# Two-layer sequence model on one core: the last batch's end in halves of two tiles, and a quarter of the low one-hots made by GpSimd and gathered last

## The chip, the cores and the metric

The kernel runs as one program on one core of one Trainium2 chip. The metric is the device time of one execution in microseconds (us). Engines are named as in the profile: PE (TensorE, matmul), PEld (its weight loads), DVE (VectorE), ACT (ScalarE), POOL (GpSimd), SP (SyncE, which only issues DMAs here). There is one core, so every semaphore wait below is between engines of the same core.

## What is computed

Input x is 4 batches of 512 tokens by 128 features. Four sublayers follow one another, each with a residual and a LayerNorm without weights. The last two matter here.

```python
# third sublayer: causal linear attention, 16 heads of 8
numer = einsum(q, cumsum(k v)); denom = max(einsum(q, cumsum(k)), 1e-6)
y = numer / denom;  x3 = layernorm(x2 + y @ w_out.T)
# fourth: product-key expert layer, 8192 rows of down and up, 8 heads, top 8
mean, var = x3 over all 2048 tokens, per feature           # batch norm
xn = (x3 - mean) * rsqrt(var + eps) * bn_gamma + bn_beta
sim = (xn @ w_q.T) . keys                                  # 2 sides x 8 heads x 32 keys
scores, idx = top_k(sim, 8)                                # first choice, per side
all_scores = scores[0][:, None] + scores[1][None, :]
sc, pk = top_k(all_scores, 8)                              # second choice, 64 rows a token
indices = 32 * idx[0] + idx[1] at pk                       # numbers below 8192
h = gelu(x3 . down[indices]) * sigmoid(sc)
out = layernorm(x3 + sum(h * up[indices]))
```

The batch norm needs the moments of all four batches, so the fourth sublayer cannot start before x3 of the last batch is done.

## The kernel before, in words

The program is two blocks, one after the other: `layers` (the first three sublayers, about 290 us of the span) and `peer` (the fourth). Within a block each engine has its own instruction list, written out by hand in a fixed order; engines meet only in semaphore waits (`wait(engine, semaphore, b, k)`). There is no planner. At the end of a block all engines wait for one another.

**End of `layers`.** A batch has T = 4 tiles of 128 tokens. The last batch (B - 1 = 3) ends with a serial chain over all four tiles: VectorE reduces the numerators (`b_summed`, line 984) and makes y (`b_y`, 988 to 993); TensorE transposes y (`b_yt`, 1428); ScalarE copies it out (502); TensorE multiplies with w_out (`b_z3`, 1435); VectorE adds x2 (`b_z3`, 1000) and takes the moments of each row (`b_z3_spread`, 791 to 796); GpSimd raises to the power -1/2 (`root`, 625); VectorE normalises to x3 (`b_x3`, 801); TensorE transposes x3 (`b_x3t`, 1443); ScalarE copies (507); VectorE takes the batch norm's moments of the copy (`b_moments`, 1016). Then `peer` begins with `bn_aggr` (2028), a root on GpSimd and, on ScalarE, `xn` (`normed`, 1770).

**`peer`.** A pair is two tiles (256 tokens); there are PAIRS = 8 pairs p, with tiles u = 2p and 2p + 1. Looking up rows of down and up is done with one-hot matmuls and no gather: a number below 8192 is split into a low part (0 to 127) and a high part (below 64). For each of the 128 chosen slots of a token ("lanes" in the code) there is a low one-hot of 128 columns and a high one-hot weighted with the sigmoid; their product over tokens' lanes, taken on TensorE, has 128 by 8 entries per token. The low one-hots of a pair are made in QB = 4 quarters of LB = 32 lanes. VectorE makes quarters 0 to 2 in one instruction each (`hot_lo`, 1970). ScalarE makes quarter 3 (`last_one_hots`, 1814 to 1827): 32 Abs activations, one per lane, then one Relu over all of them, with the Gelus of `hidden` put in between the lanes ("meanwhile") in pairs 2 to 5. In pair 7 ScalarE makes 16 of those lanes and VectorE the other 16 (`last_lanes`).

The order of one pair on each engine:

- VectorE: `one_hots(p)` (lo_last 1946, w_lo 1948, lo_t, hot_hi, hot_w, then hot_lo three times), `residual(p-1)` (moments of the output, 2019 to 2025), `second_choice` of both tiles of pair p+1 (1900, 1903), `rows_columns` (1911 to 1918), `which_side` (1924), `weigh(p)` (mix, 2007; first half after two gathered quarters, second half after four), `first_choice` of both tiles of pair p+2 (1889, 1893).
- TensorE: quarters 0, 1, 2 gathered (`gathered`, 2137) with one product of `hidden` (2084) ahead of each in pairs 2 to 5; `key_scores(2p+4)` (2073); quarter 3; `key_scores(2p+5)`; one more hidden product in pairs 2 to 5; `decoded(p+1)` (2100); `outputs(p)` (2148, 2150), which waits for o of the pair before.
- ScalarE: `decoded(p)` (1809 to 1812), `side_numbers` (1793), `last_one_hots(p)`, `normal(p-1)` (o, 1835), the copies of the two key scores (`keysims`, 1778), `sigmoids` (1801), the fourth Gelu.
- GpSimd: `root(p-1)` (1738, 1741), `numbers` (eq, 1730), `candidates` (1716, 1720). It waits for the most part.
- SP: one store of a pair's output after o.

`first_choice(u)` cannot start before the copy of `key_scores(u)`; `decoded(p+1)` waits for `numbers` and `sigmoids`; the outputs of pair 7 wait for o of pair 6.

## Time and profile before

| | |
|---|---|
| three runs | 540.2, 542.76, 550.87 us, median 542.76 |
| profiled execution | 542.56 us, span 540.8 us |
| mean granted TensorE clock | 0.766 of full speed |
| busy: PE, PEld | 390.4 us (72%), 271.0 us (50%) |
| busy: DVE, ACT, POOL | 467.1 us (86%), 300.4 us (56%), 184.5 us (34%) |
| chain that ended last | DVE 25%, PE 16%, ACT 2% of the span are named in it |

Times in a row are from the start of the span. A busy share is an average over both blocks; what bounds a pair is read from the timelines of one pair. In a timeline row the first number is the start, the second the length of the merged piece, and a bracket at its end gives the idle time of that engine ahead of it and what ended it.

### The profile page before, as it was taken

What the parts mean: (1) busy time and instruction counts of PE and PEld (TensorE: products, weight loads), DVE (VectorE), ACT (ScalarE), POOL (GpSimd) and SP (SyncE); (2) the same over time, 40 slices, a digit from 0 to 9 for tenths busy, and PEclk for the clock granted to TensorE, in tenths of its full rate; (3) what the DMA queues carried; (4) which work ended last, traced back from release to release, by engine and by line L of the source; (5) the groups of instructions that cost most, each with busy time, mean ns of one, the idle gap of its engine ahead of it and who ended that gap; (6) DMA issues with size and microseconds to landing.
All of it is one profiled execution on the core that took longest, in us unless ns stands there. A gap on an engine that the chain in (4) does not pass through costs nothing. (4 is left out here: it accounts for less than half of the span.)

```text
span 540.8 us, 16061 instructions
## 1 busy us (share of the span) xinstructions
PE 390.4 (72%) x6356; PEld 271.0 (50%) x6356; DVE 467.1 (86%) x2059; ACT 300.4 (56%) x625; POOL 184.5 (34%) x209
## 2 busy tenths in 40 slices
PE   2997579877798769776345846767887878785575
PEld 1662466555555555456342325555564545545575
DVE  5387998899978998997954999999999999999992
ACT  1433455186434754238421678483968787778551
POOL 3454229632683129423511540304040403040001
PEclk9999895999688996977555885757576765858577
DMA  4800000000000000000000000000000000000000
GB/s 93 235 34 0 1 1 2 2 1 1 1 2 1 1 1 2 1 1 1 2 1 0 1 1 4 4 14 2 4 13 2 13 3 14 2 13 2 13 3 21
DMA packets 12473, 6.95 MB, mean 13 GB/s; under 512 B 3182, under 2 KB 11758, under 8 KB 12398
## 3 DMA queue, kind: packets, MB, share of 16 engines
q1 hardware_dynamic: 11366, 5.65, 3.8%
q8 instruction: 50, 0.82, 0.6%
q10 hardware_dynamic: 1032, 0.27, 0.2%
q14 instruction: 25, 0.20, 0.1%
HBM read 4.87 MB, written 1.05 MB: 11 GB/s over the span
## 5 line engine op out<-in xcount | busy, mean ns | idle before, releaser
L1820 ACT ACTIVATE hot_last<-iota_f,lo_last 128x128 f16<-128x128 f32 x240 | 72.8, 393 | 0.3 <-DVE lo_last L1946 0.3
L2137 PE MATMUL psum<-hot_w,hot_lo 64*128 64x8 f16 x2688 | 39.7, 164 | 39.8 <-DVE hot_lo L1970 26.0
L2137 PEld LDWEIGHTS psum<-hot_w,hot_lo 64*128 64x128 f16 x2688 | 37.8, 101 | 56.4 <-DVE hot_lo L1970 29.9
L1970 DVE TENSOR_TENSOR hot_lo<-lo_t,iota_lo 128x4096 f16<-128x4096 f16 x24 | 53.5, 2285 | 0.0
L2084 PE MATMUL psum<-x3t,down_t 128*128 128x512 f32 x64 | 45.9, 842 | 1.7 <-PEq L319 1.7
L1730 POOL TENSOR_TENSOR eq<-eq,side_f 128x1024 f16<-128x1024 f16 x14 | 29.0, 2088 | 48.9 <-DVE eq L1924 48.9
L1893 DVE FIND_INDEX8 side_i<-side,keysims 128x8 uint32<-128x32 f32 x256 | 41.6, 192 | 0.0
L1300 PE MATMUL psum<-we,x1t 128*128 128x512 f32 x64 | 39.6, 731 | 2.3 <-DVE wexp L875 1.1
L1738 POOL TENSOR_TENSOR rstd<-rstd,minus_half 128x2 f32<-128x2 f32 x8 | 5.7, 707 | 104.3 <-DVE rstd L2025 104.3
L1386 PE MATMUL psum<-q_hi,k_t 32*128 32x128 f16 x256 | 21.2, 264 | 19.1 <-DVE masked L952 13.1
L679 POOL TENSOR_TENSOR s_lo<-feat,s_hi 128x512 f16<-128x512 f32 x28 | 31.7, 1159 | 8.6 <-ACT s_hi L487 8.6
L2150 PE MATMUL psum<-upw,mix 128*128 128x128 f32 x256 | 34.3, 292 | 0.0
L679 POOL TENSOR_TENSOR s_lo<-masked,s_hi 128x512 f16<-128x512 f32 x28 | 31.6, 1158 | 7.0 <-DVE x L801 3.7
L2150 PEld LDWEIGHTS psum<-upw,mix 128*128 128x128 f32 x256 | 33.3, 210 | 0.0
L2073 PE MATMUL psum<-keysim,xn 128*128 128x512 f32 x32 | 30.1, 1040 | 3.2 <-ACT keysims L1778 2.6
L889 DVE SCALAR_TENSOR_TENSOR z<-psum,wexp,z 128x128 f32<-128x128 f32 x112 | 29.6, 342 | 0.0
L1386 PEld LDWEIGHTS psum<-q_hi,k_t 32*128 32x128 f16 x256 | 12.8, 115 | 33.2 <-DVE masked L952 22.4
L487 ACT CAST s_hi<-feat 128x512 f16<-128x512 f32 x32 | 18.4, 618 | 19.5 <-PE psum L1419 14.3
L1889 DVE MAX8 side<-keysims 128x8 f32<-128x32 f32 x256 | 25.3, 187 | 3.7 <-ACT keysims L1778 3.7
L1827 ACT ACTIVATE hot_last<-hot_last 128x4096 f16<-128x4096 f16 (+1 forms) x8 | 27.2, 3404 | 0.3
L487 ACT CAST s_hi<-masked 128x512 f16<-128x512 f32 x32 | 19.2, 618 | 13.8 <-DVE masked L952 13.8
L625 POOL TENSOR_TENSOR a_rstd<-a_rstd,minus_half 128x2 f32<-128x2 f32 (+1 forms) x12 | 9.7, 805 | 49.7 <-DVE a_rstd L796 49.3
(281 smaller groups left out, 1113.2 us busy)
## 6 DMA issues: line engine op xcount, KB each, us to landing
xall<-in_L_attn_x SPq DMA_DIRECT2D x4, 256.0 KB, 4.6
out<-o SPq DMA_DIRECT2D x8, 128.0 KB, 1.8
we<-in_L_ffn_We SPq DMA_DIRECT2D x1, 512.0 KB, 4.3
downn<-in_L_ffn_down SPq DMA_DIRECT2D x1, 512.0 KB, 5.3
upw<-in_L_ffn_up SPq DMA_DIRECT2D x1, 512.0 KB, 6.3
wh<-in_L_attn_W_h SPq DMA_DIRECT2D x1, 256.0 KB, 3.2
keysn<-in_L_ffn_keys_p SPq DMA_DIRECT2D x1, 256.0 KB, 5.5
wqkv<-in_L_attn_w_qkv ACTq DMA_DIRECT2D x1, 192.0 KB
```

Source lines behind the costliest of these rows:

```text
L487: nc.scalar.copy(s_hi[:, u % 2, g, :], masked[u % 2][:, g, :]).then_inc(shi_ok.h, 1)
L679: nc.gpsimd.tensor_tensor(s_lo[:, u % 2, g, :], masked[u % 2][:, g, :], s_hi[:, u % 2, g, :], ALU.subtract).then_inc(slo_ok.h, 1)
L889: ins = nc.vector.scalar_tensor_tensor(z2[:, u, :], src, wexp[:, u, e:e + 1], (z2 if e else x1)[:, u, :], ALU.mult, ALU.add)
L1300: ins = nc.tensor.matmul(bank[Y_BANK[u] + k][:], x1t[:, P * u:P * u + P], v.we[:, 4 * k:4 * k + 4, :].rearrange("p e m -> p (e m)"), start ...
L1386: ins = nc.tensor.matmul(bank[S_BANK[b][g]][:, P * c:P * c + P], k_t[r, u, c, :], q[r, u, c, :], start=(q is q_hi), stop=(q is q_lo))
L1820: ins = nc.scalar.activation(hot_last[:, lane], iota_f[:], ACT.Abs, bias=lo_last[:, lane:lane + 1], scale=-1.0)
L1893: ins = nc.vector.max_index(side_i[:, u % 4, s, :], side[:, u % 4, s, :], keysims[:, u % 4, s, :])
L1970: nc.vector.tensor_tensor(hot_lo[:, pairs], bc(lo_t[:, lanes].rearrange("p (j s) -> p j s", s=2).unsqueeze(2), [P, LB // 2, P, 2]), bc(v.i ...
L2073: nc.tensor.matmul(bank[6][:], xn[:, P * (u % T):P * (u % T) + P], v.keysim[:].rearrange("p s k -> p (s k)"), start=True, stop=True)\
L2084: nc.tensor.matmul(bank[H_BANK(b, c)][:], v.down_t[:, c, :], v.x3t[:, N * b:N * b + N], start=True, stop=True).then_inc(h_mm.h, 1)
L2137: ins = nc.tensor.matmul(bank[2 + q // 2 * 2 + t][:, c:c + EH], low, hot_w[half, i, lane // 2, :, lane % 2], start=(lane % (2 * LB) == 0 a ...
L2150: ins = nc.tensor.matmul(outputs_of(p, t), mix[:, EH * t + e, :], v.upw[:, e, :], start=False, stop=(e == EH - 1))
```

## The change

In `layers`, the last batch is taken in halves of two tiles from y on. `b_y` takes a range of tiles; in the last batch it is called for tiles 0 and 1 right after `b_summed(1)` and for tiles 2 and 3 at the end. Transposes, copy, product, residual, moments, root, x3 and its transposes then run as two sets of half-size steps (`last_z3`, `last_yt`, `last_x3`, `last_x3t`), with banks of their own in PSUM. The moments of the batch norm are taken per half in all batches (`bn_raw` has two sets per batch), in the last one straight from PSUM, and the copy to x3t on ScalarE follows them.

In `peer`, quarter 2 of the low one-hots moves from VectorE to GpSimd: 32 `tensor_scalar` instructions a pair (`mid_one_hots`), one per lane, each comparing the row of 128 column numbers with a number per partition. GpSimd starts them when VectorE has made both of its quarters of the pair, and they come ahead of `root(p-1)`, `numbers` and `candidates` in its list. The order of the gathers on TensorE becomes 0, 1, 3, 2, for all pairs; `key_scores(2p+4)` stays ahead of the fourth gather, `key_scores(2p+5)` behind it. VectorE takes `first_choice(2p+4)` between the halves of mix. In pair 7 the products with x3 go ahead of the wait for the last mix. xn of the first batch is made in two parts, so that the first key scores need only the first. One semaphore (upw_ok) is folded into another (zeroed).

```diff
-                def b_y(b):
+                def b_y(b, tiles=slice(0, T)):
...
+                        b_summed(b, 1)
+                        b_y(b, slice(0, 2))
+                        b_summed(b, 2)
+                        b_summed(b, 3)
+                        b_y(b, slice(2, T))
+                for i in range(2):
+                    last_z3(i)
+                for i in range(2):
+                    last_x3(i)
+                for i in range(2):
+                    last_moments(i)
...
+                def last_yt(i):
+                    act.wait_ge(yt_mm.h, B + i)
+                    nc.scalar.copy(yt[:, 2 * P * i:2 * P * i + 2 * P], bank[2 + i][:, 0:2 * P]).then_inc(yt_ok.h, 1)
+                def last_x3t(i):
+                    act.wait_ge(x3t_mm.h, B + i)
+                    act.wait_ge(bn_ok.h, B + i)
+                    at = N * (B - 1) + 2 * P * i
+                    nc.scalar.copy(v.x3t[:, at:at + 2 * P], bank[i][:, 0:2 * P]).then_inc(x3t_ok.h, 1)
...
+    GATHER_ORDER = (0, 1, 3, 2)
...
+                def mid_one_hots(p):
+                    pool.wait_ge(lo_last_ok.h, p + 1)
+                    wait(pool, hot_ok, p)
+                    for lane in range(LB):
+                        ins = nc.gpsimd.tensor_scalar(hot_mid[:, lane], iota_f[:], lo_last[:, lane:lane + 1], None,
+                                                      ALU.is_equal)
+                    ins.then_inc(hot_mid_ok.h, 1)
...
                 for p in range(-1, PAIRS):
+                    if p >= 0:
+                        mid_one_hots(p)
                     if p >= 1:
                         root(p - 1)
...
-                    for q in range(QB - 1):
+                    for q in range(QB - 2):
...
                     if p >= 0:
-                        weigh(p)
+                        weigh(p, (0,))
                     if p + 2 < PAIRS:
-                        for u in (2 * p + 4, 2 * p + 5):
-                            first_choice(u)
+                        first_choice(2 * p + 4)
+                    if 0 <= p < PAIRS - 1:
+                        weigh(p, (1,))
+                    if p + 2 < PAIRS:
+                        first_choice(2 * p + 5)
...
+                    if p == PAIRS - 1:
+                        for t in range(2):
+                            nc.tensor.matmul(outputs_of(p, t), ident[:], v.x3[:, 2 * p + t, :], start=True, stop=False)
...
-                    for q in range(QB - 1):
-                        for c in early[q:q + 1]:
+                    for i, q in enumerate(GATHER_ORDER[0:QB - 1]):
+                        for c in early[i:i + 1]:
                             hidden(p // PB + 1, c)
                         gathered(p, q)
                     if p + 2 < PAIRS:
                         key_scores(2 * p + 4)
-                    gathered(p, QB - 1)
+                    gathered(p, GATHER_ORDER[QB - 1])
                     if p + 2 < PAIRS:
                         key_scores(2 * p + 5)
```

## Rows read from the trace of the kernel before

**Rows 1.** Chain of waits: starts of w_lo, pairs 0, 1, 2, 6 (start, length, what)

```profile
321.27 0.20 DVE w_lo L1948
...
348.54 0.20 DVE w_lo L1948
...
376.39 0.20 DVE w_lo L1948
...
492.14 0.20 DVE w_lo L1948
```

**Rows 2.** Timeline of VectorE, pair 3 (start, length, line, operation, count, idle before)

```profile
407.56 6.69 DVE L1970 TENSOR_TENSOR hot_lo<-lo_t,iota_lo 128x4096 f16<-128x4096 f16 x3
...
421.03 1.29 DVE L1924 TENSOR_TENSOR eq<-rc,iota_r 128x1024 f16<-128x1024 f16 x2
...
424.50 1.29 DVE L2007 TENSOR_TENSOR mix<-psum,hid 128x512 f32<-128x512 f32 x2 [0.98 <-PE psum L2137]
...
434.08 0.19 DVE L1946 SCALAR_TENSOR_TENSOR lo_last<-hi_t,number 128x32 f32<-128x32 f16 x1
```

**Rows 3.** Timeline of TensorE, pair 3: third gather, key scores, fourth gather

```profile
417.50 1.87 PE L2137 MATMUL psum<-hot_w,hot_lo 64*128 64x8 f16 x128
419.30 2.07 PE L2073 MATMUL psum<-keysim,xn 128*128 128x512 f32 x2
422.59 1.87 PE L2137 MATMUL psum<-hot_w,hot_last 64*128 64x8 f16 x128 [1.22 <-issue]
```

**Rows 4.** Timeline of ScalarE, pair 3: Relu, o, copy of the key scores

```profile
418.87 3.62 ACT L1827 ACTIVATE hot_last<-hot_last 128x4096 f16<-128x4096 f16 x1
422.39 0.79 ACT L1835 ACTIVATE o<-psum,shift,rstd 128x128 f32<-128x128 f32 x2
423.08 0.58 ACT L1778 COPY keysims<-psum 128x512 f32<-128x512 f32 x1
```

**Rows 5.** Timeline of ScalarE: the Relu of pairs 0 and 1

```profile
332.05 3.62 ACT L1827 ACTIVATE hot_last<-hot_last 128x4096 f16<-128x4096 f16 x1
...
358.40 3.62 ACT L1827 ACTIVATE hot_last<-hot_last 128x4096 f16<-128x4096 f16 x1
```

**Rows 6.** Groups of GpSimd by line and form (count, busy us, mean ns, idle before)

```profile
L1716 POOL TENSOR_TENSOR cand<-side 128x128 f32<-128x128 f32 x16 | 6.6, 413 | 37.9 <-DVE side L1889 37.9
...
L1738 POOL TENSOR_TENSOR rstd<-rstd,minus_half 128x2 f32<-128x2 f32 x8 | 5.7, 707 | 104.3 <-DVE rstd L2025 104.3
...
L1752 POOL TENSOR_SCALAR upw<-upw 128x1024 f32<-128x1024 f32 x1 | 2.8, 2787 | 0.1
L1741 POOL TENSOR_TENSOR shift<-shift,rstd 128x2 f32<-128x2 f32 x8 | 1.6, 197 | 0.6
```

**Rows 7.** One line's instructions on GpSimd: ns min/median/max, 128x512

```profile
L646 POOL TENSOR_SCALAR heads_t<-qk_t,gam,bet x8: 763/796/1302, 15.0 to 174.8; 128x512 f32<-128x512 f32 x8
```

**Rows 8.** Timeline of ScalarE, pair 6: table load and sigmoids

```profile
506.34 1.28 ACT L1801 ACT_TABLE_LOAD   x1
507.63 0.40 ACT L1801 ACTIVATE weight<-best 128x64 f32<-128x64 f32 x2
```

**Rows 9.** Timeline of TensorE: decoding of pair 7, first x3 products of its outputs

```profile
511.44 1.03 PE L2100 MATMUL psum<-ident_row,eq 128*128 128x128 f16 x8 [2.91 <-DVE eq L1935]
...
530.11 0.76 PE L2148 MATMUL psum<-x,ident 128*128 128x128 f32 x2 [1.20 <-DVE mix L1998]
```

**Rows 10.** Timeline of VectorE, pair 7: its three quarters

```profile
518.58 6.70 DVE L1970 TENSOR_TENSOR hot_lo<-lo_t,iota_lo 128x4096 f16<-128x4096 f16 x3
```

**Rows 11.** Timeline of VectorE: end of the last batch, the three waits

```profile
283.70 0.69 DVE L1000 TENSOR_TENSOR z<-x,psum 128x512 f32<-128x512 f32 x1 [3.96 <-PE psum L1435]
...
287.03 1.11 DVE L801 TENSOR_SCALAR x<-z,b_mv,b_rstd 128x128 f32<-128x128 f32 x4 [1.12 <-POOL b_rstd L625]
...
289.33 0.69 DVE L1016 BATCH_NORM_STATS2 bn_raw<-x3t 128x6 f32<-128x512 f32 x1 [1.19 <-ACT x3t L507]
```

**Rows 12.** Timeline of ScalarE: xn of the first batch

```profile
292.16 0.81 ACT L1770 ACTIVATE xn<-x3t,bn_shift,bn_scale 128x512 f32<-128x512 f32 x1 [1.13 <-DVE bn_shift L2038]
```

More of the change, by code:

```diff
@@ L613, in _ @@
                         b_values(a, 0)
-                    b_yt(b)
+                    if b < B - 1:
+                        b_yt(b)
                     if a + 1 < B:
@@ L1599, in _ @@
                             b_numerators(b, u)
-                    b_yt(b)
-                    if a + 1 < B:
-                        a_qk(a + 1)
-                        a_rest(a + 1)
-                    b_z3(b)
-                b_x3t(B - 1)
+                    if b < B - 1:
+                        b_yt(b)
+                        if a + 1 < B:
+                            a_qk(a + 1)
+                            a_rest(a + 1)
+                        b_z3(b)
+                for i in range(2):
+                    last_z3(i)
+                for i in range(2):
+                    last_x3t(i)
 def peer(nc, v):
@@ L1769, in normed @@
                         wait(act, ksim_mm, T * b - 1)
-                    nc.scalar.activation(xn[:], v.x3t[:, N * b:N * b + N], ACT.Identity, bias=bn_shift[:],
-                                         scale=v.bn_scale[:]).then_inc(xn_ok.h, 1)
+                    for part in (slice(0, N),) if b else (slice(0, P), slice(P, N)):
+                        nc.scalar.activation(xn[:, part], v.x3t[:, N * b:N * b + N][:, part], ACT.Identity,
+                                             bias=bn_shift[:], scale=v.bn_scale[:]).then_inc(xn_ok.h, 1)
                 def key_scores(u):
@@ L1819, in last_one_hots @@
                     for lane in range(ACT_LANES(p)):
-                        ins = nc.scalar.activation(hot_last[:, lane], iota_f[:], ACT.Abs, bias=lo_last[:, lane:lane + 1],
+                        ins = nc.scalar.activation(hot_last[:, lane], iota_f[:], ACT.Abs, bias=lo_last[:, LB + lane:LB + lane + 1],
                                                    scale=-1.0)
@@ L1994, in weigh @@
                     if p == PAIRS - 1:
-                        for q in range(QB):
-                            wait(dve, g_mm, p, q + 1)
+                        for i, q in enumerate(GATHER_ORDER):
+                            wait(dve, g_mm, p, i + 1)
                             lanes = slice(LB * q, LB * q + LB)
@@ L2002, in weigh @@
                         return
-                    for half in range(2):
+                    for half in halves:
                         wait(dve, g_mm, p, 2 * half + 2)
@@ L2068, in key_scores @@
                 def key_scores(u):
-                    wait(pe, xn_ok, u // T)
+                    pe.wait_ge(xn_ok.h, u // T + 2 if u else 1)
                     if u:
@@ L2135, in gathered @@
                                 half, c = slice(HK * t, HK * t + HK), EH * (lane % (2 * LB))
-                                low = hot_lo[half, lane // 2, :, lane % 2] if q < QB - 1 else hot_last[half, lane - LB * q, :]
+                                if q < QB - 2:
+                                    low = hot_lo[half, lane // 2, :, lane % 2]
+                                else:
+                                    low = (hot_mid, hot_last)[q - (QB - 2)][half, lane - LB * q, :]
                                 ins = nc.tensor.matmul(
                                     bank[2 + q // 2 * 2 + t][:, c:c + EH], low, hot_w[half, i, lane // 2, :, lane % 2],
-                                    start=(lane % (2 * LB) == 0 and i == 0), stop=(i == 1), skip_group_check=True)
+                                    start=(lane == LB * q and q in (0, 3) and i == 0), stop=(i == 1), skip_group_check=True)
                     ins.then_inc(g_mm.h, 1)
```

109 lines of the change are left out of this document (75 added, 34 removed).

## The prediction

> **What bounds the kernel now.** The profiled execution took 542.56 us (span 540.8), within 0.2 us of the median of the three runs, 542.76; the sum below is made against 542.56. I read the chain of waits first. In the expert layer it repeats once per pair of tiles, and the starts of w_lo mark the pairs [rows 1]: pair 0 takes 27.27 us, pair 1 27.85, pairs 2 to 5 take 115.75 together, 28.94 each, and pair 6 begins at 492.14. I write T for such a start.
>
> Then the timelines of one middle pair (T = 405.34), one engine at a time. VectorE makes three low one-hot quarters, works on, and has one visible wait, 0.98 us, before the second half of mix at 424.50; from there to the next pair's first operation at 434.08 it is busy, 9.58 us of mix and two first choices [rows 2]. That wait ends with the last quarter of gathers on TensorE, 422.59 to 424.5 [rows 3]. Those gathers could have begun at 421.37, when the key scores started at 419.30 were through; they waited for ScalarE, whose Relu over its own quarter ends at 418.87 + 3.62 = 422.49 [rows 3, 4]. So VectorE and the ScalarE-to-TensorE chain are nearly tied, and the ScalarE quarter is today hidden behind one key-score product and the third gather.
>
> **The change, part by part.** *VectorE* loses one of three hot_lo operations, 6.69 / 3 = 2.2 us a pair [rows 2], 17.7 us over eight pairs. That counts only where nothing else ends later.
>
> *Gather order 0, 1, 3, 2.* TensorE reaches its third gather at 417.50 in the middle pair [rows 3], but this is now ScalarE's quarter, not ready before 422.49. Nothing moves ScalarE earlier: its start (lo_last) and the Gelus between its lanes are as before. TensorE idles five us, gathers until about 424.5, and only then makes the key scores of tile 2p+4 that used to run at 419.30: 2.0 us more, and a ScalarE copy of 0.6 [rows 3, 4] gives 427.1. VectorE, 2.2 us ahead after its first mix half, has nothing but first_choice(2p+4) in front of it and waits for that copy. Behind it stand the second mix half and the other first choice, the same 9.58 us. So the chain 424.50 + 9.58 becomes 427.1 + 9.58: **2.6 us later, in each of pairs 2 to 5, 10.4**. In pair 0 ScalarE is done at 332.05 + 3.62 = 335.67 [rows 5]; gather 1.87, key scores 2.07, copy 0.6 give 340.2, and with 9.58 and the 0.19 of lo_last w_lo starts at 349.97 instead of 348.54: **1.4**.
>
> *The GpSimd quarter.* No row shows this operation, 128x128, one input, a scalar per partition, f16 out. From above: the single-operation scaling of upw takes 2787 ns for 1024 columns, an eighth is 0.35, and about 0.1 for starting (half of the 197 ns of a product of two columns) makes 0.45; a two-input add of just this size takes 0.41 [rows 6]. From below: the two-operation tensor_scalar on 128x512 takes 763 ns at its least, a quarter of it 0.19 [rows 7]. I take 0.33, nearer to the row of the same size since the start does not shrink with columns; 32 of them make 10.6 us. In the Trainium skill, GPSIMD Engine Reference (Performance versus the Vector engine) gives a best case of about 1.8 cycles an element at 1.2 GHz and 769 ns for 512 elements; the trace's 763 agrees. By it 128 elements are an estimated 0.19 us, the lower bound again, and the sum 549.
>
> Beside VectorE it is slower: heads_t varies from 763 to 1302 ns [rows 7]. In the middle pair the GpSimd lanes run under VectorE's which_side, 1.29 us [rows 2], and four short operations of rows_columns, about 2.1 us with both inputs in SBUF; I add 1.0 us a pair (0 to 2.1), and 0.7 in the last (0 to 1.4). In the Trainium skill, SBUF — State Buffer (Who interferes with whom) says that such a VectorE instruction and a GpSimd instruction that reads SBUF lock each other out; that would make it the whole 2.1, and the sum about 563.
>
> The quarter starts once both VectorE quarters are done, 6.7 us after T (hot_lo starts at T + 2.2, two take 4.4 [rows 2]), and is ready at T + 18.3. Queued behind it on GpSimd is root(p-1), 0.95 us with its product [rows 6], which used to run at once; behind that, on ScalarE, o of the pair before, 0.8 [rows 4], and behind o the copy of the key scores. Pairs 2 to 5: 412.05 + 10.6 + 1.0 + 0.95 + 0.8 = 425.4, under 426.5 when the key scores are there: hidden, 1.1 us to spare. The eq products of GpSimd then end near 429, before sigmoids and decoding are ready for them. Pair 1 has no Gelus in ScalarE's lanes (ready at 362.02 [rows 5], key scores through at 366.0), so here GpSimd is late: 355.24 + 11.6 + 0.95 + 0.8 = 368.6, copy 369.2, next w_lo at 379.0 instead of 376.39: **2.6**. Pair 6: the quarter is ready at 510.4, root 511.4, o 512.2, then table load 1.28 and sigmoids 0.4 [rows 8], so decoding of pair 7 starts at 513.9 instead of 511.44 [rows 9]: **2.4**. VectorE's saving there is lost to this.
>
> Pair 7 is the exposed end. Both hot_lo quarters end at 518.58 + 4.4 = 523.0 [rows 10]; with 10.6 + 0.7 the quarter is ready at 534.3. root(6) and o end at 536.0, and the outputs wait for o before their two x3 products, 0.76; the last gathers and mix (1.9 + 0.65) end at 536.9 as well. The outputs proper start at 536.8 instead of 530.87 [rows 9]; the second pair of x3 products, taken forward, gives 0.2 back: **5.7**.
>
> *The last batch in halves.* In that stretch VectorE waits 3.96 us for transposes, copy and product, 1.12 for the root, 1.19 for the transposes of x3 and their copy [rows 11], 6.3 in all. With two half chains I lay out the same steps at half size: the first half's transposes follow the last numerators at once, VectorE starts z3 at 279.6, the second at 281.6, roots end at 281.6 and 283.6, the last moments at 285.2, the ScalarE copy behind them at 285.6. Waits of 0.4, 0.75, 0.2 and 0.6 are left: about 2.0, so **4.3 saved** (2 to 6). The extra bn_stats in earlier batches, under 0.1 each, count nothing beside this. xn in two parts lets the first key scores start after a quarter of 0.81 [rows 12]: **0.4 saved**.
>
> Sum: 1.4 + 2.6 + 10.4 + 2.4 + 5.7 = 22.5, less 4.7, is +17.8: **560.4 us**.
>
> **Rivals.** (1) *GpSimd is quick*, 0.25 us or less a lane. Pair 1 then costs 0 to 0.3, pair 6 gains up to 2, the tail costs 0.9 to 2.5, but the 10.4 and 1.4 stay, since they hang on ScalarE and TensorE: 549 to 554. For: the least heads_t row. Against: upw and the cand add. Chance 0.22. (2) *GpSimd is the bound*, 0.40 us a lane or more: T + 19.5 + 1.0 + 1.75 passes the key scores in all pairs. At 0.41 with 1.0 of blocking the pairs 2 to 5 cost 4.0 each, pair 1 5.1, pair 6 4.9, the tail 8.3: 574; at 0.45, 583. For: upw, the only single-operation row. Chance 0.22. (3) *Faster*: VectorE's 2.2 us are realised in most pairs. This needs the hot_last quarter at T + 12.2, when TensorE reaches the third gather; ScalarE would have to be five us quicker than its row, for instance if TensorE's Gelu inputs were what held it. Then six pairs gain about 2 us and the halves 4.7: about 526. Against: in pair 1, with no Gelu between its lanes, it is still ready only at T + 13.5. It decides where ScalarE beats TensorE's third slot. Chance 0.07. (4) *The halves give nothing*, because the end of the layer still waits on a chain with twice as many hand-overs; the rest as forecast: 565. Chance 0.07.
>
> **Numbers.** The forecast, GpSimd between 0.26 and 0.39 a lane, has 0.42: 554 to 569. The range takes in rivals 1 and 4 and rival 2 up to 0.45 a lane: 549 to 583; outside lie 0.07 of rival 3, some of rival 2 and edges. A difference of 2% is 10.9 us, about what a measurement can tell. Slower by that, above 553.6: the forecast, rivals 2 and 4 and a little of 1, 0.70. Within: 0.22. Faster: 0.08.
>
> **What would show it.** In the changed kernel: TensorE idle about 5 us before the hot_last gathers of pairs 2 to 5, released by ScalarE; VectorE idle 5 to 6 us before the MAX8 of tile 2p+4, released by keysims; w_lo starts 31.5 us apart there; tensor_scalar on GpSimd near 0.33 us start to start; ScalarE's o late in pairs 1, 6 and 7; the last mix of pair 7 or its x3 products released by GpSimd's chain; bn_mv near 286. I am wrong if the ScalarE quarter is no longer last (periods of 27 us), or if the lanes of GpSimd cost 0.2 or 0.45.

## The result and the profile after

The changed kernel took 630.04 us, median of 4 runs (625.73 to 632.05), against 546.82 for the kernel before on the same chip (540.2 to 552.05): ratio 1.161, 95% interval 1.156 to 1.166. Medians are over all executions, while ratios, here and below, leave out those in a slower state, so a ratio is not the quotient of the two medians. The profiled execution took 625.73 (span 623.9). I had said 560.4 with a range up to 583: the sign was right, the size was off by a factor of more than four.

The page of the changed kernel, engines' busy time, the chain of waits and the first group of the costliest (busy us, mean ns, idle before):

```profile
PE 398.2 (64%) x6356; PEld 278.3 (45%) x6356; DVE 453.4 (73%) x2060; ACT 301.9 (48%) x628; POOL 341.0 (55%) x466
...
POOL 26%; DVE 21%; PE 3%; issue 1%; ACT 1%; POOLq 0%; ACTq 0%; DVEq 0%
...
L1823 POOL TENSOR_SCALAR hot_mid<-iota_f,lo_last 128x128 f16<-128x128 f32 x256 | 158.7, 647 | 76.5 <-DVE hot_lo L2066 76.5
```

One line of GpSimd now holds a quarter of the span in that chain: 256 one-hot lanes, by their records 0.65 us each in the mean and 0.61 in the median. From one start to the next it is 0.58 where nothing disturbs them, since a record ends a little after the next one's start. I had priced them at 0.33. The pair with T = 431.19 shows it, GpSimd first, then TensorE, ScalarE, VectorE:

```profile
438.11 19.56 POOL L1823 TENSOR_SCALAR hot_mid<-iota_f,lo_last 128x128 f16<-128x128 f32 x32 [8.87 <-DVE hot_lo L2066]
```

```profile
448.44 1.87 PE L2243 MATMUL psum<-hot_w,hot_last 64*128 64x8 f16 x128 [5.02 <-issue]
450.24 2.07 PE L2172 MATMUL psum<-keysim,xn 128*128 128x512 f32 x2
457.73 1.87 PE L2243 MATMUL psum<-hot_w,hot_mid 64*128 64x8 f16 x128 [5.42 <-POOL hot_mid L1823]
```

```profile
444.72 3.62 ACT L1923 ACTIVATE hot_last<-hot_last 128x4096 f16<-128x4096 f16 x1
458.68 0.81 ACT L1931 ACTIVATE o<-psum,shift,rstd 128x128 f32<-128x128 f32 x2 [10.34 <-POOL shift L1833]
459.38 0.58 ACT L1874 COPY keysims<-psum 128x512 f32<-128x512 f32 x1
```

```profile
459.99 1.59 DVE L1985 MAX8 side<-keysims 128x8 f32<-128x32 f32 x16 [12.50 <-ACT keysims L1874]
```

The fourth gather, which followed the third by five microseconds before [rows 3], is TensorE's third here and idles 5.02 us as forecast; but the key scores at 450.24 are done at 452.3, and ScalarE's copy, which stood right behind Relu and o before [rows 4], waits until 459.38, because o waits for shift and shift stands behind 32 lanes. VectorE, with 0.98 us of waiting in this pair before [rows 2], waits 12.50. The end of the program waits for the same lanes; TensorE's first gather over GpSimd's quarter in pair 7:

```profile
610.09 1.87 PE L2231 MATMUL psum<-hot_wide,hot_mid 128*128 128x16 f16 x64 [16.19 <-POOL hot_mid L1823]
```

The periods, from one w_lo to the next by the rows of the chain ("tail" is from the last w_lo to the end of the span):

```
                pair 0   pair 1   pairs 2-5, mean   pair 6   tail
before           27.27    27.85        28.94         22.53   26.1
my forecast      28.7     30.5         31.5          24.9    31.8
changed          35.75    38.53        38.53         35.04   42.0
```

The end of the last batch went as drawn: from the reduction of the second tile's sums on VectorE to bn_mv it took 15.23 us before (275.12 to 290.35) and 11.39 in the changed kernel (277.59 to 288.98). Where one wait of 3.96 stood [rows 11] there are now 0.52 and 0.69:

```profile
282.23 0.42 DVE L1045 TENSOR_TENSOR z<-x,psum 128x256 f32<-128x256 f32 x1 [0.52 <-PE psum L1499]
...
284.34 0.42 DVE L1045 TENSOR_TENSOR z<-x,psum 128x256 f32<-128x256 f32 x1 [0.69 <-PE psum L1499]
...
286.61 0.60 DVE L820 TENSOR_SCALAR x<-z,b_mv,b_rstd 128x128 f32<-128x128 f32 x2 [0.33 <-POOL b_rstd L643]
...
287.77 0.43 DVE L1060 BATCH_NORM_STATS2 bn_raw<-psum 128x6 f32<-128x256 f32 x1 [0.23 <-PE psum L1507]
```

### The profile page after: what moved, and what is told of

Its sections match the earlier page's. It is cut to its first block, busy times and chain, and to the rows that moved or that the text cites. A ratio compares the mean times of both kernels' runs of the same rounds, so it can differ in the third digit from the quotient of the medians.

```text
span 623.9 us, 16339 instructions
## 1 busy us (share of the span) xinstructions
PE 398.2 (64%) x6356; PEld 278.3 (45%) x6356; DVE 453.4 (73%) x2060; ACT 301.9 (48%) x628; POOL 341.0 (55%) x466
## 4 chain that ended last, share of the span: by engine, by line
POOL 26%; DVE 21%; PE 3%; issue 1%; ACT 1%; POOLq 0%; ACTq 0%; DVEq 0%
POOL hot_mid L1823 25%; DVE side_i L1989 6%; DVE hot_lo L2066 6%; DVE side L1985 4%; DVE hot_w L2053 1%; DVE mix L2103 1%; PE psum L2261 1%; DVE hot_hi L2046 1%; POOL rstd L1830 1%; PE psum L2172 1%; PE psum L2243 1%; ACT keysims L1874 1%; ACT o L1931 0%; DVE hot_wide L2059 0%; DVE best_i L1999 0%
## 5 line engine op out<-in xcount | busy, mean ns | idle before, releaser
L1823 POOL TENSOR_SCALAR hot_mid<-iota_f,lo_last 128x128 f16<-128x128 f32 x256 | 158.7, 647 | 76.5 <-DVE hot_lo L2066 76.5
L1931 ACT ACTIVATE o<-psum,shift,rstd 128x128 f32<-128x128 f32 x16 | 6.5, 454 | 102.1 <-POOL shift L1833 102.1
L2243 PE MATMUL psum<-hot_w,hot_mid 64*128 64x8 f16 x896 | 13.1, 165 | 49.6 <-POOL hot_mid L1823 49.6
L2243 PE MATMUL psum<-hot_w,hot_lo 64*128 64x8 f16 x1792 | 26.4, 164 | 25.4 <-DVE hot_lo L2066 18.0
L2243 PEld LDWEIGHTS psum<-hot_w,hot_lo 64*128 64x128 f16 x1792 | 25.0, 100 | 35.8 <-DVE hot_lo L2066 21.9
L2243 PEld LDWEIGHTS psum<-hot_w,hot_mid 64*128 64x128 f16 x896 | 12.5, 101 | 59.1 <-POOL hot_mid L1823 59.1
L2243 PE MATMUL psum<-hot_w,hot_last 64*128 64x8 f16 x896 | 13.2, 164 | 35.8 <-issue 30.7
L2066 DVE TENSOR_TENSOR hot_lo<-lo_t,iota_lo 128x4096 f16<-128x4096 f16 x16 | 35.9, 2283 | 0.0
L697 POOL TENSOR_TENSOR s_lo<-masked,s_hi 128x512 f16<-128x512 f32 x28 | 31.6, 1160 | 7.0 <-DVE x L820 3.7
L2243 PEld LDWEIGHTS psum<-hot_w,hot_last 64*128 64x128 f16 x896 | 12.8, 101 | 42.2 <-issue 42.2
L2103 DVE TENSOR_TENSOR mix<-psum,hid 128x512 f32<-128x512 f32 x28 | 17.9, 678 | 17.5 <-PE psum L2243 17.5
```

Of the source, the lines that this page charges most:

```text
L697: nc.gpsimd.tensor_tensor(s_lo[:, u % 2, g, :], masked[u % 2][:, g, :], s_hi[:, u % 2, g, :], ALU.subtract).then_inc(slo_ok.h, 1)
L1823: ins = nc.gpsimd.tensor_scalar(hot_mid[:, lane], iota_f[:], lo_last[:, lane:lane + 1], None, ALU.is_equal)
L2066: nc.vector.tensor_tensor(hot_lo[:, pairs], bc(lo_t[:, lanes].rearrange("p (j s) -> p j s", s=2).unsqueeze(2), [P, LB // 2, P, 2]), bc(v.i ...
L2103: nc.vector.tensor_tensor(mix[:, EH * t:EH * t + EH, lanes], bank[2 + 2 * half + t][:].rearrange("p (l e) -> p e l", e=EH), hid[:, b % 2, ...
L2243: ins = nc.tensor.matmul(bank[2 + q // 2 * 2 + t][:, c:c + EH], low, hot_w[half, i, lane // 2, :, lane % 2], start=(lane == LB * q and q i ...
```

## The experiments

My theory: the sum stands except for the price of a lane. Rivals: contention with VectorE makes the lanes slow; the new order, or what queues behind the lanes, costs by itself. Ratios are against the kernel before on the same chip, with 95% intervals.

### The halves alone

The expert layer is that of before; only the last batch's halves and the two-part xn are kept.

```
-    GATHER_ORDER = (0, 1, 3, 2)          (and all that goes with hot_mid)
+    quarters 0, 1, 2 by VectorE, gathers 0, 1, 2, 3
```

> The kernel before with only the last batch's end in halves and xn in two parts; the expert layer's orders, and all one-hots, as before. My theory (the excess of the changed kernel is all GpSimd's quarter; the halves save what the trace of the changed kernel shows between the numerators of tile 1 and the first bn_mv, 11.4 us instead of 15.2, and 0.4 for xn): 4.2 us faster than before, ratio near 0.992, and the time from that reduction to bn_mv is 11.4 us. Rival (the layer's part also became slower, since in the changed kernel the same reduction came 2.5 us later than before): 1 to 2 us faster, ratio 0.996 to 1.0, with that reduction again 2 us or more later than before.

Measured: 544.04, ratio 0.9965 [0.9919, 1.001]. The stretch is 11.39 us, the same as in the changed kernel, so 3.8 us are saved there; the whole kernel shows about 2, not told apart from nothing. My 4.2 us were missed, and what the rival had named is there: about 2 us, and the reduction at 277.55, 2.4 us later than before. But that place moves from execution to execution: kernels with the same halves have it anywhere from 273.4 (the new order without GpSimd) to 281.9 (half the share). The tail was 27.4 instead of 26.1 in the profiled execution, nearly all of it in the last 32 products with up: 5.0 us at a mean granted clock of 0.78 before (530.7 to 535.7), 6.3 us at 0.61 here (527.3 to 533.6). The halves are not the loss.

### The new order without GpSimd

```
-                    if p >= 0:
-                        mid_one_hots(p)
...
-                    for q in range(QB - 2):
+                    for q in range(QB - 1):     (VectorE makes quarter 2; order 0, 1, 3, 2 kept)
```

> The changed kernel with one part undone: VectorE makes quarter 2 again, as before, GpSimd does nothing new. The gather order 0, 1, 3, 2, the split first choices, the x3 products ahead and the halves stay. My theory (order alone costs 2.6 us in each of pairs 2 to 5 and 1.4 in pair 0, since the key scores now wait behind ScalarE's quarter): w_lo starts 31.5 us apart in pairs 2 to 5, TensorE idle 5 us before the gathers of hot_last, total 6 to 7 us slower than before, ratio 1.012. Rival (the order costs nothing once GpSimd is out of it, the reordered first choice fills the wait): periods of 29 us or less there, 4 to 5 us faster than before, ratio 0.991.

Measured: 556.91, ratio 1.0196 [1.0152, 1.024], some 12 us over the halves alone in the same comparison, and more than the 1.012 that I expected. Pairs 2 to 5 take 31.9 in the mean (w_lo from 374.89 to 502.57), but they are not alike: pairs 2 to 4 take 31.5 to 31.6, which is my 31.5, and pair 5 takes 33.0. VectorE's wait for the copy of the key scores, in pair 4 and in pair 5:

```profile
459.73 1.59 DVE L1971 MAX8 side<-keysims 128x8 f32<-128x32 f32 x16 [3.62 <-ACT keysims L1860]
...
492.77 1.59 DVE L1971 MAX8 side<-keysims 128x8 f32<-128x32 f32 x16 [5.06 <-ACT keysims L1860]
```

The 3.62 are the 0.98 that VectorE waited before [rows 2] and 2.6 for the order. The step with ScalarE's quarter ahead of the key scores stands. Pair 5 has more because TensorE pauses inside its gather of ScalarE's quarter, after 95 of the 128 matmuls. The same happens in pair 1, after 113; this pair takes 30.3 against 27.85 before, where I had put nothing for the order:

```profile
362.08 0.35 PE L2225 MATMUL psum<-hot_w,hot_last 64*128 64x8 f16 x15 [2.27 <-issue]
...
489.52 0.59 PE L2225 MATMUL psum<-hot_w,hot_last 64*128 64x8 f16 x33 [1.89 <-issue]
```

### The quarter in one GpSimd instruction

One subtraction over the whole quarter in place of 32 comparisons; what it writes is not one-hots, only the time is asked.

```
-                    for lane in range(LB):
-                        ins = nc.gpsimd.tensor_scalar(hot_mid[:, lane], iota_f[:], lo_last[:, lane:lane + 1], None,
-                                                      ALU.is_equal)
+                    ins = nc.gpsimd.tensor_tensor(hot_mid[:], bc(iota_f[:].unsqueeze(1), [P, LB, P]),
+                                                  bc(lo_last[:, 0:LB].unsqueeze(2), [P, LB, P]), ALU.subtract)
```

> The changed kernel, but GpSimd makes its quarter with one tensor_tensor subtract over 128x4096 in place of 32 tensor_scalar; the comparison itself is left out, so the values are no one-hots. My theory (price and queue of the quarter are what costs, and the two-input form runs at 2.0 to 2.3 ns a column, 8.4 to 9.3 us in all): the quarter is ready 16 us after w_lo, hidden behind ScalarE's in pairs 2 to 5, periods there 31.5 us, total 550 to 558 us in the terms of 542.6 before, ratio 1.015 to 1.03. Rival (any GpSimd work in this slot holds VectorE's two-input operations back or is slowed by them): the instruction takes 12 us or more, or VectorE's rows_columns start several us late, total above 565, ratio above 1.04.

Measured: 569.98, ratio 1.0435 [1.0378, 1.0492], not the theory's 550 to 558 but the rival's range. The instruction is shorter than I expected, but VectorE stands still beside it:

```profile
415.34 7.03 POOL L1822 TENSOR_TENSOR hot_mid<-iota_f,lo_last 128x4096 f16<-128x4096 f32 x1 [8.84 <-DVE hot_lo L2065]
415.64 0.25 DVE L2117 BATCH_NORM_AGGREGATE mv<-stats 128x2 f32<-128x6 f32 x2
415.92 6.48 DVE L2119 TENSOR_SCALAR shift<-mv 128x2 f32<-128x2 f32 x1
```

A tensor_scalar of two columns takes 6.48 us on VectorE, 0.17 in the kernel with lanes. So one long instruction trades GpSimd's time for VectorE's. The lanes, each short, hold nobody up for long.

### A price list

Behind the last pair of the kernel before, with VectorE done, GpSimd ran ten kinds of instruction.

```
+                for _ in range(4):
+                    nc.gpsimd.tensor_scalar(new("h"), a, s1, None, ALU.is_equal)
...              (f32 out; mult by pointer; mult by constant; mult + add; is_equal + mult;
...               512 columns; tensor_tensor of 128 and of 1024 columns)
```

> The kernel before with a list of GpSimd operations appended to the end of GpSimd's work, in forms that differ in one thing: 128 columns is_equal by a scalar per partition with f16 out, the same with f32 out, mult instead of is_equal, mult by an immediate, two operations mult and add, is_equal and mult, is_equal over 512 columns, a two-input subtract, and 8 rows of 128 in one instruction with f32 and with f16 inputs. The result is the reference's; the total time says nothing. My theory (the form is what costs: a tensor_scalar with one operation takes a slow path, as the scaling of upw did at 2.7 ns a column, and two operations the fast one): the first four at 0.45 to 0.6 us, the two-operation forms at 0.2 to 0.35. Rival (is_equal itself is slow): the mult forms at 0.3 or less with one operation too, both is_equal forms at 0.6. Second rival (contention with VectorE made the 0.6): all forms at 0.35 or less here, where VectorE is idle.

GpSimd's timeline of the first eight kinds, in the order of the cut (start, length of all, line, shape, count):

```profile
544.95 2.35 POOL L1778 TENSOR_SCALAR o_h<-t_in,t_s 128x128 f16<-128x128 f32 x4
547.27 2.33 POOL L1780 TENSOR_SCALAR o_f<-t_in,t_s 128x128 f32<-128x128 f32 x4
549.58 2.34 POOL L1782 TENSOR_SCALAR o_f<-t_in,t_s 128x128 f32<-128x128 f32 x4
551.89 2.01 POOL L1784 TENSOR_SCALAR o_f<-t_in 128x128 f32<-128x128 f32 x4
553.90 1.73 POOL L1786 TENSOR_SCALAR o_f<-t_in,t_s 128x128 f32<-128x128 f32 x4
555.61 2.79 POOL L1788 TENSOR_SCALAR o_h<-t_in,t_s 128x128 f16<-128x128 f32 x4
558.38 3.10 POOL L1790 TENSOR_SCALAR o_h<-t_in,t_s 128x512 f16<-128x512 f32 x2
561.45 1.47 POOL L1792 TENSOR_TENSOR o_h<-t_in,t_s 128x128 f16<-128x128 f32 x4
```

From start to start: the comparison 0.58 us, with f32 output too; multiplication the same (547.27 to 549.58 and on to 551.89), so the operation and the output type do not matter; multiplication by a constant 0.50; multiply then add 0.43; compare then multiply 0.69; the comparison over 512 columns 1.53. So the one-operation forms cost what my theory gave them, the two-operation forms more than its 0.2 to 0.35. One operation costs 1.53 - 0.58 = 0.95 us for 384 columns, 2.5 ns a column, and 0.26 us to start. The two-operation form takes 763 ns at 512 columns [rows 7] and 0.43 at 128: 0.87 ns a column and 0.32 to start. The Trainium skill's 769 ns for 512 elements (GPSIMD Engine Reference, Performance versus the Vector engine) agrees with the two-operation row alone. Both of my bounds left out most of the start. A quarter of 763 ns gives 0.19 where 128 columns of that form take 0.43, and that form is besides not the one used: the comparison takes 0.15 more. An eighth of upw (0.35) plus 0.1 takes the start at a third to a half of what it is. VectorE was idle here, so contention is not the price.

### rstd and shift inside the lanes

```
                    for lane in range(LB):
                        ins = nc.gpsimd.tensor_scalar(...)
+                        if lane == 12 and p >= 1:
+                            root(p - 1)
```

> The changed kernel, with GpSimd's two instructions for the previous pair's outputs (rstd, shift) issued after lane 12 of the 32 lanes instead of behind all of them. Theory (two things sit behind the lanes: the third gather of this pair, and through rstd and shift the o of the previous pair, ScalarE's copies of the key scores behind it and VectorE's first choices): the first choice no longer waits; what is left is lanes' end T+27.4, gather 2.4, mix and one first choice 5.4 to 5.9, so periods of pairs 1 to 5 fall from 38.5 to 35.2 to 35.8, pairs 6 and 7 pay 0.9 each for the later lanes: about -13 us against the changed kernel, ratio to before 1.137. Rival A (the gather alone is what waits, rstd does not matter): periods 38.5, ratio 1.16. Rival B (what is queued behind the lanes carries all of the loss): periods near 29, ratio about 1.05.

Measured: 617.94, ratio 1.1227 [1.1165, 1.1289]; periods of pairs 2 to 5 36.8. The periods and the tail add up to 11 us less than in the changed kernel, near the 13 that I expected. (The ratio shows more, but the kernel before was itself slower in this comparison, 550.96 in the median against 546.82.) ScalarE's o no longer waits for the end of the lanes, and the first choice of tile 2p+4 is done under them:

```profile
447.70 0.81 ACT L1931 ACTIVATE o<-psum,shift,rstd 128x128 f32<-128x128 f32 x2
```

It is the second tile that holds the pair now: lanes to T+27.4, as worked out, then gather, key scores of 2p+5, copy, choice, decoding, 9.2 to 9.6 us together and not the 7.8 to 8.4 of my expectation, which had the copy hidden behind mix; VectorE waits 1.2 us for it. Both chains hang on the end of the lanes; a better place in the queue does not replace a cheaper lane.

### Key scores ahead of the third gather

VectorE makes quarter 2, order 0, 1, 3, 2:

```
                        for c in early[i:i + 1]:
                            hidden(p // PB + 1, c)
+                        if i == 2 and p + 2 < PAIRS:
+                            key_scores(2 * p + 4)
                        gathered(p, q)
-                    if p + 2 < PAIRS:
-                        key_scores(2 * p + 4)
```

> The kernel in which VectorE makes the third quarter but the gathers keep the changed order (quarter 0, 1, 3, 2), with the first of the pair's two key-score matmuls moved ahead of the gather of ScalarE's quarter. Theory (the changed order costs because these key scores stand behind the gather that waits for ScalarE's Relu): VectorE's 5.1 us wait before its first choice goes, periods of pairs 2 to 5 fall from 31.5 to 28.4 to 29.0, ratio to before 0.99. Rival (the order costs because the two late gathers now lie one behind the other, or because TensorE pauses inside gathers): periods stay 31, ratio 1.02.

Measured: 550.71, ratio 0.9976 [0.9904, 1.0048]. Pairs 2 to 5 take 30.6 in the mean (376.10 to 498.38), between my two cases: 1.3 of the 3.0 us that the order costs (31.9 against 28.9 with the halves alone) are the key scores' place. Much of the rest is TensorE, which pauses inside gathers: pairs 2 and 4, with one pause of 1.2 to 1.3 us, take 29.5 and 29.8, pairs 3 and 5, with two longer ones each, 31.9 and 31.1. Its timeline in pair 3:

```profile
422.30 1.53 PE L2225 MATMUL psum<-hot_w,hot_last 64*128 64x8 f16 x103 [3.31 <-issue]
...
426.17 0.51 PE L2225 MATMUL psum<-hot_w,hot_last 64*128 64x8 f16 x25 [2.35 <-issue]
...
426.52 1.52 PE L2225 MATMUL psum<-hot_w,hot_lo 64*128 64x8 f16 x102
...
429.72 0.51 PE L2225 MATMUL psum<-hot_w,hot_lo 64*128 64x8 f16 x26 [1.68 <-issue]
```

Here "issue" stands before the 104th of 128 matmuls of a gather and before the 103rd of the next: nothing that the profile shows is waited for. The pauses belong to places in TensorE's list of instructions more than to gathers that follow closely: in pair 1 one comes after 113 matmuls of ScalarE's quarter in each kernel with the order 0, 1, 3, 2 (after 111 here), in pair 5 after 95 without GpSimd and with rstd inside, and the kernel before has them too, in pairs 0, 1 and 6. In the changed kernel pairs 2 to 5 have none that shows. What TensorE waits for there was not tested.

### The lanes started at once

```
                    pool.wait_ge(lo_last_ok.h, p + 1)
-                    wait(pool, hot_ok, p)
```

> The changed kernel with GpSimd's wait for VectorE's two quarters left out: it starts its lanes when lo_last is there (T+0.3 instead of T+6.9), beside VectorE's large instructions. Theory (32 lanes of 0.61 us are a price of the instruction, not of contention): lanes end at T+20, periods fall by 6 us to about 32.3, pair 7 by about 7: ratio to before 1.07 to 1.08. Rival (GpSimd gets nothing done, or makes VectorE wait, while VectorE runs its two-byte instructions): lanes of up to 2.4 us or VectorE's hot_lo instructions longer than 2.25 us, periods 35 to 38, ratio 1.12 to 1.16.

Measured: 614.8, ratio 1.1173 [1.1105, 1.1242], just below the rival's 1.12 to 1.16 and far from the theory. Pairs 1 to 5 take 37.0, in the rival's range: of a start 6.7 us earlier 1.5 were left. GpSimd's timeline with a window ending in VectorE's hot_lo, and the spread of its three lanes there (ns min/median/max):

```profile
425.44 7.10 POOL L1822 TENSOR_SCALAR hot_mid<-iota_f,lo_last 128x128 f16<-128x128 f32 x3 [2.12 <-DVE lo_last L2041]
```

```profile
L1822 POOL TENSOR_SCALAR hot_mid<-iota_f,lo_last x3: 1313/1318/4504, 425.4 to 428.0; 128x128 f16<-128x128 f32 x3
```

A lane that meets the two hot_lo instructions lasts 4.50 us, until both are through. VectorE keeps its pace (hot_lo 2324 ns mean, 2286 in the kernel with rstd inside, whose lanes come after it). The Trainium skill, SBUF — State Buffer (Who interferes with whom), says that whoever issues first holds the shared ports for the whole instruction; the trace agrees both ways, 4.50 us on GpSimd here and 6.48 on VectorE in the one-instruction kernel. So the changed kernel's wait for VectorE, 6.7 us long, costs it 1.5 us a pair.

Does contention explain the price of a lane in the changed kernel? In the pair with T = 431.19 the last 17 lanes run while VectorE waits, and seven earlier ones beside its rows_columns and which_side (two windows of the timeline, and the spread of the seven in ns min/median/max):

```profile
442.76 5.08 POOL L1823 TENSOR_SCALAR hot_mid<-iota_f,lo_last 128x128 f16<-128x128 f32 x7
...
447.82 9.86 POOL L1823 TENSOR_SCALAR hot_mid<-iota_f,lo_last 128x128 f16<-128x128 f32 x17
```

```profile
L1823 POOL TENSOR_SCALAR hot_mid<-iota_f,lo_last x7: 598/637/1316, 442.8 to 447.2; 128x128 f16<-128x128 f32 x7
```

The 17 go at 0.58 us from start to start, as in the price list, so contention is not the price. It does come on top: of the seven, four take longer, the longest 1.32 us beside which_side. All in all it is 19.56 less 32 x 0.58, 1.0 us a pair, just what I had put. In pair 6 one more lane takes 2.38 us beside last_numbers on VectorE, and it is 21.35 less 18.56, 2.8.

### Half the share

GpSimd 16 lanes, VectorE the other 16 of quarter 2, the rest as changed:

```
-                    for lane in range(LB):
+                    for lane in range(16):      (lanes 80 to 95; hot_lo has 80 lanes)
```

> The changed kernel with 16 of the quarter's 32 lanes made by VectorE and 16 by GpSimd, all else as changed (order 0, 1, 3, 2, GpSimd waits for VectorE, rstd behind the lanes). 16 lanes of 0.61 us are 9.8 us, near the 10.6 us that I priced 32 lanes at, so this shows the rest of my sum with the lane price right. Theory (the sum was right but for the lane price): lanes end at T+8.0+9.8 = T+17.8, then rstd and shift 0.95, o 0.8, keysims 0.6, and 9.8 to the next T: periods of pairs 1 to 5 29.9 to 31.5 (the upper end where VectorE is late for the key scores, as when it made the whole quarter), tail 31: about +8 to +17 us, ratio 1.015 to 1.03. Rival (the sum was wrong in its structure too, and the chain through GpSimd costs more than its lanes): periods 34 and more, ratio above 1.07.

Measured: 568.11, ratio 1.0335 [1.0226, 1.0444], a little above the theory, far below the rival.

```profile
421.48 10.28 POOL L1826 TENSOR_SCALAR hot_mid<-iota_f,lo_last 128x128 f16<-128x128 f32 x16 [10.00 <-DVE hot_lo L2070]
```

With 10.3 us of lanes, near the 11.6 of my sum, the periods are close to my forecast's: 28.8 and 30.4 for pairs 0 and 1 (forecast 28.7, 30.5), 31.8 for pairs 2 to 5 (31.5), 27.0 for pair 6 (24.9), tail 32.5 (31.8). Pair 6 misses by 2.1; its lanes take 12.07 us, with the lane beside last_numbers that I had not priced. The whole, 1.0335, is what I had predicted for 32 lanes. Pair 1 confirms less than it seems: it takes 30.3 without any GpSimd lane as well.

### A cheaper lane

```
-                                                      None, ALU.is_equal)
+                                                      lo_last[:, lane:lane + 1], ALU.mult, ALU.add)
```

> The changed kernel with GpSimd's lanes made by two operations (multiply, then add) instead of one comparison: 32 instructions of the same shape, in the same place, that took 0.43 us each where VectorE stood idle, against 0.61. What they write is not one-hots, so the kernel computes other numbers in that quarter; only the time is asked. Theory (the price of a lane is the whole of my error, the sum around it stands): each lane's 0.18 us counts in full, 32 x 0.18 = 5.8 us per pair in all eight pairs, periods of pairs 1 to 5 38.5 - 5.8 = 32.7, about -46 us, ratio to before 1.076. That is also what my sum gave for a lane of 0.43 (two thirds of the way from 574 to 583 at 0.41 and 0.45: 579 against 543, 1.067). Rival (with shorter lanes another wait takes over, VectorE's or TensorE's own pauses): periods 34 and more, ratio above 1.10.

Measured: 594.01, ratio 1.0925 [1.0841, 1.1008]. Periods and tail add up to 37 us less than in the changed kernel, not the 46 that I expected, because the 32 lanes took 15.11 us in place, not 13.8:

```profile
428.03 15.11 POOL L1823 TENSOR_SCALAR hot_mid<-iota_f,lo_last 128x128 f16<-128x128 f32 x32 [8.87 <-DVE hot_lo L2066]
```

That is 19.56 - 15.11 = 4.45 us less, and the period of pairs 2 to 5 is 34.06, 4.47 less than 38.53. A microsecond off the lanes is a microsecond off the pair, in pairs 0 to 6; the tail fell by 5.4 with 4.8 off its lanes. No other wait took over. My expectation had two errors: I took 0.61, the length of a record, less 0.43, a time from start to start, where 0.58 less 0.43 is 0.15 a lane, and I left out contention, 1.35 us here.

### Smaller shares, for a faster kernel

Halves, order 0, 1, 2, 3, GpSimd starts at once with some lanes of VectorE's third quarter (GV) and of ScalarE's (GA):

```
+    GV, GA = 8, 8        (sixteen lanes), 4, 4 (eight), 8, 4 (twelve)
+    V_LANES = P - LB - GV
...
-                    wait(pool, hot_ok, p)
-                    for lane in range(LB):
+                    for lane in range(GV + GA):
```

> The halves, and GpSimd with 16 lanes instead of 32: 8 of VectorE's third quarter and 8 of ScalarE's quarter, started when lo_last is there, gathers in the order 0, 1, 2, 3. Theory (the share was wrong, not the idea: 16 x 0.61 = 9.8 us end at T+10.2, before VectorE is done with its own quarters, and both VectorE and ScalarE get shorter): periods of pairs 2 to 5 fall from 28.9 to about 27.4, with the halves' 4 us about -12 us, ratio to before 0.978. Rival (GpSimd beside VectorE's large instructions makes these longer by as much as the 8 lanes save, or is itself held up to the third gather): periods 29 to 30, ratio 1.0 to 1.01.

Measured: 569.48, ratio 1.0346 [1.0301, 1.0391], worse than the rival. The lanes started at T and yet took 16.67 us, since GpSimd got only two of them done under VectorE's three hot_lo (4.50 and 1.86 us); in the pair with T = 386.31 they end at 403.16, the third gather comes at 403.27, and rstd and o behind them.

```profile
386.49 16.67 POOL L1825 TENSOR_SCALAR hot_mid<-iota_f,lo_last 128x128 f16<-128x128 f32 x16 [2.10 <-DVE lo_last L2044]
```

> The halves, and GpSimd with 8 lanes, 4 of VectorE's third quarter and 4 of ScalarE's, started when lo_last is there, gathers in the order 0, 1, 2, 3. GpSimd stood still while VectorE ran its hot_lo instructions in the sixteen-lane kernel, so 8 lanes end at T+0.2+6.6+8 x 0.61 = T+11.7, before the third gather (T+12.3) and only 1.6 us after the previous pair's rstd could start, which nobody needs before ScalarE's Relu ends. Theory (the share was wrong, not the idea): VectorE saves 0.28 us per pair and its 0.98 us wait for ScalarE goes, periods of pairs 1 to 5 fall by 1.2, with the halves -10 us: ratio 0.982. Rival (nothing is to be had: VectorE and TensorE's own pauses bound the pair): ratio as with the halves alone, 0.995.

Measured: 538.85, ratio 0.987 [0.9789, 0.9952]: faster than the kernel before. In the pair with T = 399.14 the eight lanes end at 410.9, before the third gather at 411.49:

```profile
399.32 11.56 POOL L1825 TENSOR_SCALAR hot_mid<-iota_f,lo_last 128x128 f16<-128x128 f32 x8 [2.09 <-DVE lo_last L2044]
```

Pairs 2 to 5 take 28.4 against 28.94 [rows 1], half of the saving that I expected; pair 1 takes 28.2 against 27.85, a loss. ScalarE, with four lanes fewer, does not end earlier: its timeline shows a Gelu between the lanes waiting 3.00 us for TensorE, and Relu ending at 416.64, T+17.5, against T+17.2 before [rows 4]. VectorE still waits 0.49 for the key scores' copy.

```profile
407.85 0.60 ACT L1883 ACTIVATE hid<-psum 128x512 f32<-128x512 f32 x1 [3.00 <-PE psum L2186]
...
413.45 3.19 ACT L1925 ACTIVATE hot_last<-hot_last 128x3584 f16<-128x3584 f16 x1
```

Later places for the Gelus among the 28 lanes might give more; that was not run. Against the halves alone (0.9965, another comparison) the intervals overlap, so the share's own part is not shown by the times alone. By the traces it is 0.5 us a pair in pairs 2 to 5 and 2.0 in all, 218.4 us from the first w_lo to the end against 220.4.

> The same with 12 lanes, 8 of VectorE's and 4 of ScalarE's. Lanes end at T+14.1, 1.8 us after the third gather could start and before ScalarE's quarter is ready (T+15.6). Theory (a gather that starts before ScalarE's quarter is ready costs nothing): periods fall by 1.5 us in pairs 1 to 5, ratio 0.98. Rival (the third gather, held up, comes right before the fourth, and TensorE pauses between them): periods 29 to 30, ratio 1.0.

Measured: 546.92, ratio 0.9952 [0.9891, 1.0013]. In time, twelve lanes give nothing that can be told apart from the halves alone; the 1.5 us a pair that I expected did not come. By the trace, pairs 2 to 5 take 28.4 as with eight lanes, but pairs 0 and 1 and the tail are longer, and from the first w_lo to the end it is 222.7, 2.3 more than with the halves alone. With sixteen it is 245.3. So the small gain of eight lanes is gone at twelve.

## Why the prediction was wrong

**The step that failed** is the term "The GpSimd quarter": "I take 0.33". The instruction takes 0.58 us from start to start, in place and by itself, above my upper bound of 0.45, and 32 of them with contention 19.56 us instead of 10.6 + 1.0. I had noted the condition ("if the lanes of GpSimd cost 0.2 or 0.45") but let the range end at 0.45, since I built both bounds by dividing long instructions and left out most of the start, and the lower one from a form with two operations, whose columns take 0.87 ns against 2.5. Rival 2, GpSimd as the bound, is what happened, beyond its end.

**The rest of the sum, redone with 19.56.** Pairs 2 to 5: 412.05 + 19.56 + 0.95 + 0.8 + 0.6 + 9.58 + 0.19 = 443.73, less T = 405.34, is 38.4; measured 38.53. Pair 1: 355.24 + 31.68 = 386.9, period 38.4; measured 38.53. Pair 6, with its 21.35: ready at 520.2, o, table load and sigmoids to 523.6, and 3.2 of decoding as before (511.44 to w_lo at 514.67): 34.7; measured 35.04. Pair 7: the lanes end at 542.6, gathers and mix at 545.2, outputs 14.3 late; the measured tail is 15.9 longer. Pair 0 I had priced without GpSimd. Its lanes end at T+26.84, and 8.9 follow, as in the kernel with rstd inside (35.33 less 26.41): 35.75. This one is read from the traces, not worked out ahead. Together 8.5 + 10.5 + 37.8 + 12.2 + 14.3 = 83.3, less 4.7, gives 621.2 against 625.73. Of the missing 4.5, 2.5 lie ahead of the change (the same reduction at 277.59 instead of 275.12) and 1.6 in the tail, 1.0 of it in the last 32 products (6.0 us at a granted clock of 0.61, 5.0 at 0.78 before). Smaller differences go both ways.

**ScalarE's quarter and the key scores**: right. TensorE's wait of 5.02 us is there with and without GpSimd's quarter, and without it pairs 2 to 4 take the 31.5 us of the forecast. What I had put at nothing are TensorE's pauses inside the gather of ScalarE's quarter, which make it 33.0 in pair 5 and cost 2.5 us in pair 1. For pair 1 I had 2.6 from GpSimd's lateness; that the number also fits the kernel without GpSimd is luck. In the changed kernel all of this is hidden under the larger cost.

**"Hidden, 1.1 us to spare"**, for root and o behind the lanes, was the most fragile sentence: the spare time was smaller than the error of a price multiplied by 32. It turned into the 12.50 us wait.

**Contention**: right in size and place for pairs 2 to 5, 1.0 a pair priced and 1.0 measured, beside rows_columns and which_side. In pair 7 it was 1.0 against 0.7, and in pair 6 2.8 against 1.0, since I had not thought of last_numbers. By itself it would have been harmless.

**The halves**: 4.3 priced, 3.84 measured in the stretch (1.77 us of waits against my 2.0, and a wait at the barrier of 0.77 instead of 0.33, which I had not counted). xn in two parts took VectorE's wait for the first key scores from 3.73 to 3.36, 0.37 against 0.4. The time of the whole kernel does not show it beyond its uncertainty.

**VectorE's 17.7 us off** bought nothing, as forecast: its busy share fell to 73% and it waited for the copies.

## What to carry to other kernels

Before a piece of work is cut into N small instructions on another engine, get the price of one at its own size and with its own operands: the start cost is multiplied by N, and dividing a long instruction leaves it out. If two rows for the same engine, put on one size, disagree by more than a factor of two, they are likely different forms with different prices, and the range must go beyond both. Then look at what is queued behind the moved work on its new engine: spare time there must be larger than N times the doubt about one instruction. A share fitted to the time in which the engine is really free (8 lanes, not 32) cost nothing and by its trace saved 2 us, which the times alone do not show, where the full share lost 16%. And one price is compared with another only if both are read the same way: a record's length (0.61) is not the time from start to start (0.58).

## What the runs showed of the hardware that was not expected

- GpSimd's tensor_scalar with one operation is slower than with two: 0.58 us against 0.43 at 128 columns, 1.53 at 512 against 0.76 [rows 7]. But a comparison followed by a multiplication takes 0.69. A tensor_tensor of 128 columns takes 0.36. All are times from start to start but the 0.76, a record's length.
- A short VectorE instruction was held for 6.48 us by one of GpSimd's, and a GpSimd lane for 4.50 by VectorE's hot_lo: in both the one that was running was not interrupted. The lane had to sit out two hot_lo, of which the second started while it waited.
- TensorE pauses of 1.7 to 2.4 us inside a gather, after 92 to 113 of its 128 matmuls, put down to "issue", at nearly the same place of the program in different kernels; shorter ones, and others elsewhere in a gather, are there too.
- The part of the kernel that no edit touches moves by up to 8 us between profiled executions: the reduction at 277.59 in the changed kernel lies at 273.38 with VectorE's quarter and at 281.40 with the cheaper lane. A term of 4 us, as the halves', is therefore read from its own stretch.
